# Last attention of a four-layer kernel: value products of four heads per step instead of two

## What is computed

```python
def _qdq(x):
    s = jnp.maximum(jnp.max(jnp.abs(x), axis=-1, keepdims=True) / 127.0, 1e-08)
    return jnp.clip(jnp.round(x / s), -127.0, 127.0) * s
# per batch: q = qdq(norm(x)) @ wq + bq;  k, v from the context, made in an earlier stage
# per head h: p_h = softmax(q_h @ k_h.T / sqrt(32));  o_h = p_h @ v_h
# x = x + qdq(o) @ wp + bp
```

## Time and profile before

| what | value |
|---|---|
| median of 3 runs | 2215.29 us (2210.61 to 2215.78) |
| profiled execution, its own time | 2214.09 us |
| span of its trace | 2212.3 us |
| PE busy | 2062.1 us (93%) |
| DVE busy | 1121.0 us (51%) |
| ACT busy | 826.5 us (37%) |
| mean granted TensorE clock | 0.975 of full |
| `attention3` on PE | from about 1780 to 2002 us of the span |
| line 2420, value products | 768 records |

### The profile page before, as it was taken

How to read it: one execution, slowest core, us unless ns; L and a number is a source line. 1 busy time by engine, 2 the same in 40 slices (tenths; PEclk the granted TensorE clock), 3 DMA queues, 4 the chain that set the end, 5 groups by cost and what they waited for, 6 DMA issues and landing times.

```text
span 2212.3 us, 28740 instructions
## 1 busy us (share of the span) xinstructions
PE 2062.1 (93%) x10661; PEld 1168.5 (53%) x10684; DVE 1121.0 (51%) x2469; ACT 826.5 (37%) x1717; POOL 181.4 (8%) x466
## 2 busy tenths in 40 slices
PE   8999999999999798999999999999488888888999
PEld 3444444444666344555555555566244445556665
DVE  1324554258121485555555555487355568774221
ACT  1232233321111264445444455355232235553331
POOL 0011110000000121101110110010100100000000
PEclk9999999999999999999999999999799989998999
DMA  5354442451641511120000011300100502220000
GB/s 227 130 209 174 163 155 103 193 207 60 212 138 59 196 57 42 38 89 21 22 22 22 22 29 40 135 18 10 37 16 15 177 29 88 81 64 10 11 11 15
DMA packets 60315, 185.13 MB, mean 84 GB/s; under 512 B 10578, under 2 KB 29010, under 8 KB 54463
## 3 DMA queue, kind: packets, MB, share of 16 engines
q1 hardware_dynamic: 58451, 145.55, 19.1%
q0 software_dynamic: 1728, 37.75, 4.4%
HBM read 124.61 MB, written 49.50 MB: 79 GB/s over the span
## 4 chain that ended last, share of the span: by engine, by line
PE 71%; DVE 15%; issue 5%; ACT 4%; DMA 2%; POOL 1%; SPq 1%; DVEq 0%; POOLq 0%; ACTq 0%
PE psum L120 47%; PE psum L113 8%; PE psum L1558 5%; PE psum L2612 4%; PE psum L1603 4%; DVE R L654 3%; ACT R L583 2%; DVE small L2491 2%; DVE R L653 1%; PE psum L1146 1%; DVE R L1313 1%; PE psum L2420 1%; DMA d_kv<-WK 1%; DVE R L1312 1%; DVE WK L2497 1%
## 5 line engine op out<-in xcount | busy, mean ns | idle before, releaser
L120 PE MATMUL psum<-R,WK 128*125 128x512 f32 (+10 forms) x3144 | 1084.3, 491 | 34.3 <-DMA WK<-in_ctxT 7.9
L120 PEld LDWEIGHTS psum<-R,WK 128*112 128x112 f32 (+4 forms) x3158 | 516.7, 172 | 545.3 <-issue 421.5
L113 PE MATMUL psum<-small,WK 112*125 112x112 f32 (+5 forms) x2036 | 286.3, 271 | 77.8 <-DVE WK L1303 20.1
L113 PEld LDWEIGHTS psum<-small,WK 112*125 112x125 f32 (+5 forms) x2036 | 225.0, 155 | 185.3 <-issue 76.6
L120 PE MATMUL psum<-WK,R 128*32 128x128 f32 (+5 forms) x1880 | 221.9, 354 | 25.6 <-DMA WK<-d_cd 12.0
L1734 DVE TENSOR_REDUCE small<-psum 112x1 f32<-112x487 f32 x128 | 85.1, 665 | 194.2 <-PE psum L120 190.3
L120 PEld LDWEIGHTS psum<-WK,R 128*32 128x32 f32 (+4 forms) x1880 | 120.2, 135 | 107.7 <-issue 46.8
L1558 PE MATMUL psum<-R,WK 128*112 128x512 f32 x256 | 120.1, 592 | 0.0
L1653 ACT ACTIVATE WK<-psum,small 112x487 f32<-112x487 f32 x128 | 96.9, 757 | 54.2 <-DVE small L1736 53.2
L1603 PE MATMUL psum<-R,WK 125*128 125x448 f32 (+1 forms) x256 | 107.6, 543 | 0.0
L1646 ACT ACTIVATE WK<-WK,small 112x487 f32<-112x487 f32 x128 | 90.0, 703 | 45.8 <-DVE small L1728 45.7
(11 more groups left out here) (237 smaller groups left out, 2137.6 us busy)
## 6 DMA issues: line engine op xcount, KB each, us to landing
R<-in_wf POOLq DMA_DIRECT2D x6, 4096.0 KB, 13.8
d_w<-R POOLq DMA_DIRECT2D x6, 2048.0 KB, 18.1
R<-d_w SPq DMA_DIRECT2D x6, 2048.0 KB, 11.1
WK<-in_ctxT SPq DMA_DIRECT2D x16, 750.0 KB, 6.7
d_v<-WK SPq DMA_DIRECT2D x16, 750.0 KB
R<-in_wq SPq DMA_DIRECT2D x7, 1024.0 KB, 8.0
R<-in_wo SPq DMA_DIRECT2D x6, 1024.0 KB, 15.0
d_k<-X SPq DMA_DIRECT2D x8, 750.0 KB, 5.2
```

Source lines behind the costliest of these rows:

```text
L113: ins = pe.transpose(dst, src, idn[0:k, 0:k])
L120: ins = pe.matmul(dst, lhs, rhs, start=k == 0, stop=k == len(pairs) - 1)
```

## The change

The value products of two pairs are now made together, at the odd pair's step: four heads, one in each of the four groups of 32 output partitions, 12 products in a row instead of twice 6. The even pairs' steps `o` do nothing. The turned probabilities therefore wait one step longer, and `probT` has four slots by pair (`j % 4`). Its new size does not fit in WK, so it is laid at the start of R0, over `wd`; ACT and DVE wait for the store of `wd` at the start of the stage.

```diff
-            probT = A.get(4 * NS * T, rows=SP, s=2, j=2, i=NS, t=T)
+            probT = Area(R0).get(8 * NS * T, rows=SP, s=4, j=2, i=NS, t=T)
...
-                        elif kind == "o":
-                            if j == 0:
+                        elif kind == "o" and j % 2:
+                            if j == 1:
...
                             even_ring.wait_drained(pe, b, f"pT{2 * j}")
                             odd_ring.wait_drained(pe, b, f"pT{2 * j + 1}")
                             for t in range(NS):
-                                for a in range(2):
-                                    h = 2 * j + a
-                                    ins = pe.matmul(o_ring.bank["o"][h % 4 * HW:(h % 4 + 1) * HW,
-                                                                     h // 4 * T:(h // 4 + 1) * T],
-                                                    V[b % 2][:, t, h * HW:(h + 1) * HW], probT[:, j % 2, a, t, :],
+                                for a in range(4):
+                                    h = 2 * (j - 1) + a
+                                    ins = pe.matmul(o_ring.bank["o"][a * HW:(a + 1) * HW, h // 4 * T:(h // 4 + 1) * T],
+                                                    V[b % 2][:, t, h * HW:(h + 1) * HW],
+                                                    probT[:, h // 2 % 4, a % 2, t, :],
                                                     start=t == 0, stop=t == NS - 1)
...
             def act(act):
+                act.wait_ge(sem("spline_wd_stored"), 16)
...
-                            act.copy(probT[:, j % 2, 1], odd_ring.bank[f"pT{h}"][0:SP, 0:NS * T]
+                            act.copy(probT[:, j % 4, 1], odd_ring.bank[f"pT{h}"][0:SP, 0:NS * T]
...
                 x_ready(dve, n)
+                dve.wait_ge(sem("spline_wd_stored"), 16)
...
-                            dve.tensor_copy(probT[:, j % 2, 0], even_ring.bank[f"pT{h}"][0:SP, 0:NS * T]
+                            dve.tensor_copy(probT[:, j % 4, 0], even_ring.bank[f"pT{h}"][0:SP, 0:NS * T]
```

## The result

| | before | changed |
|---|---|---|
| median | 2213.66 us (4 runs, 2210.61 to 2215.78) | 2236.23 us (4 runs, 2231.84 to 2259.11) |
| profiled execution | 2214.09 us | 2236.38 us |
| span of its trace | 2212.3 us | 2234.6 us |
| mean granted clock | 0.975 | 0.956 |

A forecast was written before the change was run, and what follows sets the result against it. DVE was taken to set the pace of middle batches, with two crossings over PE. Emptied places gave -2.8 us and clock falls +12.1 us: +9.3 us, 2224.6 us on the median's scale, range 2211 to 2237 us.

The forecast's parts named there:

- which places lie on the chain: In a middle batch, only the value blocks of pairs 3 and 5 lie on the chain of waits.
- the middle batches' gain of 0: Four places of 0.70 us emptied per middle batch, none on the chain: gain 0, at most 4 x 0.70 us.
- Rival B: PE sets the pace after all: six middle batches gain 16.8 us more, 2195.7 us; chance 0.04.
- four heads cost what two cost: At line 2420, a 24-record block adds 0 us over a 12-record one; at most 0.70 us more.
- rival C: Groups three and four don't overlap: each four-head block costs 0.70 us more, 2225.1 us in all; chance 0.04.
- the pauses: PE's waits in middle batches grow from 0.68 to 1.38 us, and from 0.73 to 1.2 us followed by 0.5.
- the cause: Longer PE pauses and less PE work let the granted clock fall to 0.50 in most middle batches, about six times.
- the price per microsecond: With PE the bound at the low clock, each us there loses 0.297 us in middle batches.
- A fall of 6.8 us loses 2.0 us ... Six: +12.1 us.: Clock falls in middle batches: +12.1 us; bounds 0 and +24.2 us, the latter for six falls of 13.6 us.
- Last batch and drain ... 2.2 us: Three emptied blocks and a merged double block at the end save 2.2 us; bounds 0 and 2.8 us.
- the -2.8 us: Gain outside the middle batches: 0.6 us in the first batch plus 2.2 us in the last batch and drain.
- what was said of pair 3's place: Its value block lies on a middle batch's chain, ahead of turned queries and product `y`; the change keeps it.

The follow-up runs named there:

- experiment 7: Only pair 6's products moved, into pair 7's block, against the kernel before: 2231.94 us, ratio 1.0086.
- experiment 9: Pairs 0 and 5 moved, into the blocks of pairs 1 and 6, against the kernel before: 2210.65 us, ratio 1.0.
- experiment 4: Only pair 5's products moved, into pair 6's block with four slots, against the kernel before: 2205.92 us, ratio 0.9972.
- experiment 1: The changed kernel with unused filler products put back in the four emptied places: 2213.44 us, ratio 1.0005 to the kernel before.
- experiment 2: The kernel before with the even pairs' value products left out, nothing else changed: 2246.13 us, ratio 1.0129.
- experiment 8: The changed kernel with filler at pairs 4 and 6 only, pairs 0 and 2 empty: 2220.42 us, ratio 1.0052 to the kernel before.
- experiment 6: Only pair 3's products moved, into pair 4's block, against the kernel before: 2233.03 us, ratio 1.0083.
- experiment 10: Pairs 1 and 5 moved, into the blocks of pairs 2 and 6, against the kernel before: 2213.2 us, ratio 1.001.

## Why the prediction was right, and where it was wrong

**Right: which places lie on the chain, and the middle batches' gain of 0.** No batch of the changed kernel is without a fall, but part of one is: from the y addition at 1902.14, past the emptied places of pairs 4 and 6, to the turning at 1912.29 it ran at full clock and took 10.15 us, where the same stretch of before (1860.99 to 1871.13) took 10.14. Rival B would have had 1.4 us less there, and is out. In experiment 7 the batch at full clock took 25.50 us without pair 6's place, and in experiment 9 pair 0's place gave 0.04 us beside pair 5's (24.76 against 24.80). Pair 2's place was not seen by itself at the full clock. Experiment 4 shows it from the other side: the place that the prediction named as on the chain (pair 5) gives its 0.72 us as soon as it is emptied.

**Right: four heads cost what two cost.** 24 records last 0.78 us, 12 lasted 0.77. The groups of instructions of the changed kernel, line 2420 (busy us and mean ns of one, then idle before):

```profile
L2420 PE MATMUL psum<-R 125*32 125x112 f32 x768 | 33.0, 320 | 0.6 <-ACT R L2458 0.6
```

The count is the one forecast, the busy time 33.0 us and not 26, because many of its blocks ran at the low clock (1.35 us at 1917.68, above). A third and fourth group cost 0.01 us at the full clock, as rows 4 had it; rival C is out. The rule of the Trainium skill that was weighed against this ("TensorE: Matmul & The Clock Gate", "Part 3: Packing small matmuls — row/col tiling": weight loads overlap running products only where the row groups differ) is not what these rows show: in the 0.71 us from 1909.43 PE's products were busy for 0.71 and its weight loads for 0.54 us, all on the same 125 rows. The measurement decides.

**Right: the pauses.** Forecast at p = 0 was 1.38 us; measured, 1.38. Forecast at p = 3 were 1.2 us and then about 0.5 us; measured, 1.26 and 0.30. Behind the pair at p = 3 the clock fell, here and in experiment 7, where only pair 6's place was emptied.

**Right: the cause, and the price per microsecond.** Refilling the places takes the loss away (experiment 1); emptying them by leaving work out, with no other part of the change, brings it (experiment 2). In the five batches of 27.3 to 31.5 us, 61.4 us at the low clock cost 17.0 us, 0.277 us each; in experiment 8, 10.5 us for 37.4, 0.28 each. Forecast was 0.297. The rule of the Trainium skill on brief pauses between groups of products (same page, "A second HAM failure mode: psum-queue depth-cycling") agrees: the clock did go back and forth here.

**Wrong: "A fall of 6.8 us loses 2.0 us ... Six: +12.1 us."** This is the term that was mis-sized, by the length of a fall and not much by their number. In the middle there were seven falls, not six, and their mean length was 10.7 us: two of 20.5 us beside five of 6.8. That is 75.0 us at the low clock, not 41. Up to 1983.98 they cost 3.0 + 17.0 = 20.0 us, where the sum had 12.1 - 0.6 = 11.5. The bound of 13.6 us per fall held for their sum (81.6 us), and with it the range.

**Wrong: "Last batch and drain ... 2.2 us".** The sum took this off and let the clock there stay as it was. From 1983.98 to the end the changed kernel lost 1.4 us instead. PE's pause ahead of the fall in the last batch had grown too, from 1.32 us to 1.75, and the fall lasted 17.1 us where it had lasted 6.8: 10.3 us more at the low clock, for which the sum had no term. All the low time in the prediction's own sum gives 85.3 x 0.297 - 2.8 = 22.5 us, against the 22.3 us between the profiled executions; part of that agreement is luck, since each us cost 0.277 in the middle and the -2.8 us are not shown.

What led to the short length: rows 8 offered two, 6.8 us of the fall at 1981.1 and 20.4 us of the first batch, and I took the shorter for all. In the short one PE was busy for 6.70 of 6.70 us, in the long one for 16.89 of 20.40. The prediction gives no reason for leaving the long one out of the sum. In the changed kernel PE is busy for 6.70 of 6.70 us in the short stretches and 20.40 of 20.40 us in the long ones, so that busy time alone doesn't say when the clock comes back. What does was not found.

**Wrong: what was said of pair 3's place.** It is on the chain, but emptying it gives 0.05 us (experiment 6), since the odd bank's copy is as late as the block is long. The prediction used just this wait for `xiT` in the first batch and did not look for it at `qT`. It carried no term, as the change keeps that block.

**Not settled.** The -2.8 us of the ends are not shown by themselves. Up to the first y addition the changed kernel lost 3.0 us in the stage with 13.6 us more at the low clock, whose price would be 3.8 to 4.0 us; a gain of 0.6 us or somewhat more fits, but that is an argument and no measurement. In the drain, falls lie over everything. And what decides that a given pause lets the clock fall is open: experiment 6 has the same 1.92 us of work with either outcome, one batch apart, and so has experiment 7 the same two pauses.

## What to carry to other kernels

Before work is taken off an engine, ask whether its place lies on the chain of waits, and, where it does, what the next instruction would wait for once the place is empty: of the places emptied here one gave anything (pair 5's), and pair 3's, on the chain too, did not, because a copy behind it was just as late. Work off the chain can carry something: on PE it kept the granted clock up, and one block of 0.7 us per batch emptied off the chain (experiment 7) cost 0.9% of the whole kernel. So read the granted clock by windows of the stage, of before and after, with the idle gaps that grow; and where falls must be priced, take their length from the longest that the trace shows as well as from the shortest.

## What the hardware showed that was not expected

The clock stays low while PE is busy all the time: stretches of 3.4 to 30.7 us were seen, the longest with PE busy for 30.60 of 30.60 us. It falls after 20.40 us in which PE was busy for 16.28 us, with pauses of 1.26 and 0.30 us at the end, and also after pauses of only 0.71 and 0.62 us. The same pauses one batch earlier left it alone, in experiment 6 and in experiment 7. Kernels at this edge spread widely from run to run (35 us in 12 runs of experiment 10, 16 us in 12 of experiment 9, 5 us in 7 with pair 5 alone), with the mean granted clock of each run going along; but the kernel before, too, spread over 14 us in the 19 runs beside experiment 10. And 20 small filler records whose results nobody reads (0.75 us, experiment 1) took back the whole loss, though they too are work that PE must do.
